# An RWKV-6 layer inside a sixteen-part kernel: one straight-line front, 32 scan units of 16 keys by 8 values, values spread by DMA, and a norm by a centring product

## The reference, cut to what matters

```python
delta = shifted - x                      # x one token back, minus x
xp = tanh((x + delta * mu0) @ W_x0.T)    # 160 columns, five groups of 32
mus = einsum(xp, W_x2) + x_bias          # one mix per kind: r, w, k, v, g
r, k, v, g = ((x + delta * mu) @ W.T)    # 64, 64, 128, 128 columns
w = tanh((x + delta * mu_w) @ W_w1.T) @ W_w2.T + b_w2
# per head h of 4, key i of 16, value j of 32, token t:
o[t, j] = sum_i r[t, i] * (S[i, j] + u[i] * k[t, i] * v[t, j])
S[i, j] = exp(-exp(w[t, i])) * S[i, j] + k[t, i] * v[t, j]
o = (o - mean) * rsqrt(var + eps)        # over the 32 values of a head
x = x + (o * gn_weight + gn_bias) * silu(g) @ W_o.T
```

## Time and profile before

| | |
|---|---|
| median of 3 runs | 3856.74 us (3844.39 to 3859.89) |
| the profiled execution, its own time | 3816.58 us |
| its span | 3814.8 us |
| granted clock of TensorE, mean | 0.864 |
| busy: PE, DVE, ACT, POOL | 3021.5, 2024.3, 1374.9, 670.1 us |
| from this layer's layernorm to its last sum | 2479.1 to 2832.1 us of the span |

### The profile page before, as it was taken

How to read it: one execution, slowest core, us unless ns; L and a number is a source line. 1 busy time by engine, 2 the same in 40 slices (tenths; PEclk the granted TensorE clock), 3 DMA queues, 4 the chain that set the end, 5 groups by cost and what they waited for, 6 DMA issues and landing times. The chain is left out here.

```text
span 3814.8 us, 57392 instructions
## 1 busy us (share of the span) xinstructions
PE 3021.5 (79%) x22522; PEld 1598.0 (42%) x22522; DVE 2024.3 (53%) x3730; ACT 1374.9 (36%) x2632; POOL 670.1 (18%) x561
## 2 busy tenths in 40 slices
PE   6566877788887699897688889977878658867986
PEld 4454247323475244444222224422233443654555
DVE  5211254588753788203788771166763453536643
ACT  3211434623243366423567762210102112223652
POOL 0000017065354100004443200000000000240003
PEclk9666869788888799999899999978789679977997
DMA  2022002022012321000311000000000000023202
GB/s 103 14 66 63 0 19 56 16 94 66 17 47 80 72 40 28 1 0 13 66 30 29 2 1 0 10 0 0 0 0 0 1 0 21 25 56 77 48 15 67
DMA packets 81292, 118.55 MB, mean 31 GB/s; under 512 B 12743, under 2 KB 51623, under 8 KB 79763
## 3 DMA queue, kind: packets, MB, share of 16 engines
q1 hardware_dynamic: 74003, 100.67, 10.6%
q0 software_dynamic: 7040, 14.43, 1.4%
HBM read 90.04 MB, written 24.81 MB: 30 GB/s over the span
## 5 line engine op out<-in xcount | busy, mean ns | idle before, releaser
L1674 DVE TENSOR_REDUCE at_mp<-PS 128x1 f32<-128x384 f32 (+3 forms) x640 | 313.3, 538 | 115.3 <-PE PS L1524 99.0
L1624 ACT ACTIVATE at_pt<-PS 128x384 f32<-128x384 f32 (+3 forms) x704 | 288.4, 456 | 212.8 <-PE PS L1536 177.6
L1521 PE MATMUL PS<-at_kx,at_qx 72*128 72x384 bf16 (+5 forms) x640 | 218.4, 346 | 67.7 <-DMA at_kx<-L_attn_a_parts 26.7
L1534 PE MATMUL PS<-at_qx,at_kx 105*128 105x512 bf16 (+5 forms) x704 | 214.8, 315 | 8.0 <-ACT at_pt L1624 6.0
L3860 ACT ACTIVATE ls_pt<-PS,ls_far 128x512 f32<-128x512 f32 x256 | 155.4, 684 | 23.1 <-PE PS L3681 18.6
L4007 DVE CUSTOM_DVE_ANT_0 PS<-PS,ls_pt 128x1024 f32<-128x1024 f32 x128 | 153.8, 1240 | 18.1 <-ACT ls_pt L3860 15.1
L2287 DVE TENSOR_TENSOR_SCAN mb_ring<-PS,mb_ring 128x1024 f32<-128x1024 f32 x64 | 146.6, 2291 | 18.9 <-POOL mb_ring L2226 6.7
L2242 PE MATMUL PS<-mb_ring,ident 128*128 128x512 f32 x256 | 147.7, 729 | 6.0 <-DVE mb_ring L2292 6.0
L1536 PE MATMUL PS<-at_above,identb 128*128 128x128 bf16 x704 | 134.1, 223 | 0.0
L2271 ACT ACTIVATE PS<-mb_dt,mb_a 128x1024 f32<-128x1024 f32 x64 | 71.6, 1118 | 168.1 <-DVE mb_ring L2287 168.1
L1521 PEld LDWEIGHTS PS<-at_kx,at_qx 102*128 102x128 bf16 (+1 forms) x640 | 64.5, 101 | 161.3 <-DVE at_mp L1674 85.6
(11 more groups left out here) (820 smaller groups left out, 6787.0 us busy)
## 6 DMA issues: line engine op xcount, KB each, us to landing
dl_arena<-in_fir_bank SPq DMA_DIRECT2D x32, 256.0 KB, 3.2
lnA<-mb_rows SPq DMA_DIRECT2D x16, 512.0 KB, 3.7
XN<-mb_rows SPq DMA_DIRECT2D x16, 512.0 KB, 3.7
ffn_place<-in_ffn_L SPq DMA_DIRECT2D x4, 1152.0 KB, 17.2
at_qx<-L_attn_a_parts SPq DMA_DIRECT2D x24, 192.0 KB
at_kx<-L_attn_a_parts SPq DMA_DIRECT2D x72, 64.0 KB
at_qx<-L_attn_b_parts SPq DMA_DIRECT2D x24, 192.0 KB
at_kx<-L_attn_b_parts SPq DMA_DIRECT2D x72, 64.0 KB
```

The costliest lines, as they stand in the source:

```text
L1521: mm = nc.tensor.matmul(PS[:, n % 3, 0:e - c], QX[0:RAW, u % 3, g, blk(i, P)], KX[0:RAW, u % 3, g, c:e], start=True, stop=True)
L1534: mm = nc.tensor.matmul(PS[:, 3 + n % 3, 0:e - c], KX[0:FULL, u % 3, g, blk(j, P)], QX[0:FULL, u % 3, g, c:e], start=True, stop=True)
L1624: nc.scalar.activation(PT[:, y % SLOTS, g, 0:e - c], PS[:, 3 + n % 3, 0:e - c], ACT.Exp, scale=SCALE).then_inc(exp_done, 1)
L1674: nc.vector.tensor_reduce(best, sc, AX.X, ALU.max).then_inc(s_maxed, 1)
```

## The change

Only `l2a` is changed. It has three stages in place of ten passes through five, no loop, and no split into bfloat16 parts:

- The front works on four blocks of 512 tokens. PE's order is a pipeline over steps s: `narrow` of block s, `mix` of s - 1, `project` of s - 2, `finish` of s - 3. ACT keeps the projections, POOL adds XN to each mix, and SP writes V to a DRAM tensor `rw_v_rows`.
- The recurrence has 32 units. A unit holds 16 keys by 8 values of one head on the 128 partitions, so four units in a row belong to one head and use the same spread of k, decay and r, made by float32 products with SEL once per head. SP fetches the 8 value rows, each to 16 partitions, in four buffers; POOL multiplies them by the spread key, which ACT has copied to SBUF; DVE scans and multiplies by r; PE sums the keys with a shifted 0/1 matrix RED, and at the end of a sequence adds the bonus VB.
- The norm works on four blocks of 512: a product with CM = I - BM centres, ACT takes Square, then Ln and Exp(-0.5 x) for the reciprocal root, DVE has two fused instructions and the sum.

POOL builds SEL (128 x 512 float32, two affine selects), RED (16 affine selects of 8 columns) and CM beside the layernorm.

```diff
+        arena = sb("rw_arena", [P, 20 * BLK])
...
+        KS = [k.XN[:, i * SEQ:(i + 1) * SEQ] for i in range(2)]
+        SS = [k.lnA[:, 0:SEQ], k.lnA[:, SEQ:2 * SEQ]]
...
+            own(pool.tensor_tensor(CM[:, :], k.ident[:, :], BM[:, :], ALU.subtract))
...
+            for d in range(DK):
+                own(pool.affine_select(out=v, in_=v, compare_op=ALU.not_equal, fill=1.0, base=-VG * d, pattern=[[-1, VG]], channel_multiplier=1))
...
+            @block.sync
+            def _(sp):
+                for b in range(NBLK):
+                    sp.wait_ge(p_kept, KINDS * b + V_KEPT)
+                    sp.dma_start(v_rows[:, blk(b)], V[:, blk(b)]).then_inc(stored, 16)
+                sp.wait_ge(stored, 16 * NBLK)
...
+                def narrow(b):
+                    pe.wait_ge(xx0_done, b + 1)
+                    if b:
+                        pe.wait_ge(xp_done, 2 * b)
...
+                for s in range(NBLK + 3):
+                    if s < NBLK:
+                        narrow(s)
+                    if 0 <= s - 1 < NBLK:
+                        mix(s - 1)
+                    if 0 <= s - 2 < NBLK:
+                        project(s - 2)
+                    if 0 <= s - 3 < NBLK:
+                        finish(s - 3)
...
+                        pool.wait_ge(mixed, KINDS * b + i + 1)
+                        pool.tensor_tensor(XX[:, b % 2, i, :], XX[:, b % 2, i, :], k.XN[:, blk(b)], ALU.add).then_inc(xx_done, 1)
...
+                for u in range(UNITS):
+                    s, j = u // GROUPS, u % GROUPS
+                    if u >= 4:
+                        sp.wait_ge(kv_done, u - 3)
+                    sp.dma_start(VS[u % 4], v_rows[VG * j:VG * j + VG, s * SEQ:(s + 1) * SEQ].unsqueeze(0).to_broadcast([DK, VG, SEQ])).then_inc(spread[u % 4], 16)
...
+                    if u >= 3:
+                        pool.wait_ge(scanned, u - 2)
+                    pool.tensor_tensor(KV[u % 3], VS[u % 4], KS[g % 2], ALU.mult).then_inc(kv_done, 1)
...
+                def decays(g):
+                    if g:
+                        pe.wait_ge(scanned, PER_HEAD * g)
+                    lines(g, 2, slice(64, P), RD[64:P, :], d_ready)
+
+                def receptance(g):
+                    if g:
+                        pe.wait_ge(sr_done, PER_HEAD * g)
+                    lines(g, 4, slice(0, 64), RD[0:64, :], r_ready)
...
+                for u in range(UNITS):
+                    g = u // PER_HEAD
+                    last = u % PER_HEAD == PER_HEAD - 1 and g + 1 < SPREADS
+                    if last:
+                        decays(g + 1)
+                        receptance(g + 1)
+                    add(u)
+                    if last and g + 2 < SPREADS:
+                        keys(g + 2)
...
+                    nc.vector.tensor_tensor_scan(SS[u % 2], wide(2), KV[u % 3], 0.0, ALU.mult, ALU.add).then_inc(scanned, 1)
+                    dve.wait_ge(scanned, u + 1)
+                    dve.wait_ge(r_ready, g + 1)
+                    if u >= 2:
+                        dve.wait_ge(o_added, u - 1)
+                    nc.vector.tensor_tensor(SR[u % 2][:, 1:], SS[u % 2][:, 0:SEQ - 1], wide(4)[:, 1:], ALU.mult).then_inc(sr_done, 1)
...
+                def root(b):
+                    act.wait_ge(var_ready, b + 1)
+                    if b >= 2:
+                        act.wait_ge(normed, b - 1)
+                    nc.scalar.activation(RS[:, b % 2, :], PS[:, 4 + b % 2, :], ACT.Ln, bias=k.eps_col[:, 0:1]).then_inc(log_done, 1)
+                    act.wait_ge(log_done, b + 1)
+                    nc.scalar.activation(RS[:, b % 2, :], RS[:, b % 2, :], ACT.Exp, scale=-0.5).then_inc(root_done, 1)
+
+                square(0)
+                square(1)
+                for b in range(NBLK):
+                    root(b)
+                    if b + 2 < NBLK:
+                        square(b + 2)
...
+                    nc.vector.scalar_tensor_tensor(out=O[:, blk(b)], in0=PS[:, b, :], scalar=W[pre + "gn_weight"], in1=RS[:, b % 2, :], op0=ALU.mult, op1=ALU.mult).then_inc(normed, 1)
```

More of the change, by code:

```diff
@@ new lines, in l2a @@
+        XX = rows(0, 10).rearrange("p (a i n) -> p a i n", a=2, i=KINDS)
+        DX, XX0, XP, XP5, RU = (rows(10 + 2 * i, 2).rearrange("p (a n) -> p a n", a=2) for i in range(5))
+        T64 = k.lnA[0:64, 0:2 * BLK].rearrange("p (a n) -> p a n", a=2)
+        VS = [rows(2 * i, 2) for i in range(4)]
+        KV = [rows(8 + 2 * i, 2) for i in range(3)]
+        SR = [rows(14 + 2 * i, 2) for i in range(2)]
+        KS = [k.XN[:, i * SEQ:(i + 1) * SEQ] for i in range(2)]
+        SS = [k.lnA[:, 0:SEQ], k.lnA[:, SEQ:2 * SEQ]]
@@ L2335, in layer_constants @@
+        O = V
+        SQ, RS = (rows(2 * i, 2).rearrange("p (a n) -> p a n", a=2) for i in range(2))
+        v_rows = nc.dram_tensor("rw_v_rows", (P, NTOK), F32).ap()
+        wide = lambda a: PS[:, a:a + 2, :].rearrange("p a b -> p (a b)")
         def layer_constants(pool, own):
-            own(pool.memset(XS[:, 0:1], 0.0))
-            own(pool.memset(SS[:, 0:1], 0.0))
             head_constants(k, pool, own, BM[:, :], 1.0 / 32)
+            own(pool.tensor_tensor(CM[:, :], k.ident[:, :], BM[:, :], ALU.subtract))
@@ L2340, in layer_constants @@
             own(pool.memset(SEL[:, :, :], 0.0))
-            v = SEL[:, :, :].rearrange("q d (h v) -> q d h v", v=32)
+            v = SEL[:, :, :].rearrange("q h (d v) -> q h d v", v=VG)
             for part in range(2):
-                own(pool.affine_select(out=v, in_=v, compare_op=ALU.not_equal, fill=1.0, base=-64 * part, pattern=[[-1, DK], [-DK, 4], [0, 32]], channel_multiplier=1))
+                own(pool.affine_select(out=v, in_=v, compare_op=ALU.not_equal, fill=1.0, base=-64 * part, pattern=[[-DK, HEADS], [-1, DK], [0, VG]], channel_multiplier=1))
@@ new lines, in l2a, with _, variance, out @@
+        with stage(nc, "centered", "squared", "var_ready", "log_done", "root_done", "normed", "gated", "y_ready", "added") as (
+                block, centered, squared, var_ready, log_done, root_done, normed, gated, y_ready, added):
+            @block.tensor
+            def _(pe):
+                def variance(b):
+                    pe.wait_ge(squared, b + 1)
+                    if b >= 2:
+                        pe.wait_ge(log_done, b - 1)
+                    nc.tensor.matmul(PS[:, 4 + b % 2, :], BM[:, :], SQ[:, b % 2, :], start=True, stop=True).then_inc(var_ready, 1)
+                def out(b):
+                    pe.wait_ge(gated, b + 1)
+                    if b >= 2:
+                        pe.wait_ge(added, b - 1)
+                    nc.tensor.matmul(PS[:, 6 + b % 2, :], W[pre + "W_o"], O[:, blk(b)], start=True, stop=True).then_inc(y_ready, 1)
+                for b in range(NBLK):
+                    nc.tensor.matmul(PS[:, b, :], CM[:, :], O[:, blk(b)], start=True, stop=True).then_inc(centered, 1)
+                variance(0)
+                variance(1)
+                for b in range(NBLK):
+                    if b + 2 < NBLK:
+                        variance(b + 2)
+                    out(b)
+            @block.scalar
+            def _(act):
+                def square(b):
+                    act.wait_ge(centered, b + 1)
+                    if b >= 2:
+                        act.wait_ge(var_ready, b - 1)
+                    nc.scalar.activation(SQ[:, b % 2, :], PS[:, b, :], ACT.Square).then_inc(squared, 1)
+                def root(b):
+                    act.wait_ge(var_ready, b + 1)
+                    if b >= 2:
+                        act.wait_ge(normed, b - 1)
[4 more added lines that the diff above has]
+                square(1)
+                for b in range(NBLK):
+                    root(b)
+                    if b + 2 < NBLK:
+                        square(b + 2)
+            @block.vector
+            def _(dve):
+                def norm(b):
+                    dve.wait_ge(root_done, b + 1)
+                    nc.vector.scalar_tensor_tensor(out=O[:, blk(b)], in0=PS[:, b, :], scalar=W[pre + "gn_weight"], in1=RS[:, b % 2, :], op0=ALU.mult, op1=ALU.mult).then_inc(normed, 1)
+                    dve.wait_ge(normed, b + 1)
+                    nc.vector.scalar_tensor_tensor(out=O[:, blk(b)], in0=O[:, blk(b)], scalar=W[pre + "gn_bias"], in1=G[:, blk(b)], op0=ALU.add, op1=ALU.mult).then_inc(gated, 1)
+                def add(b):
+                    dve.wait_ge(y_ready, b + 1)
+                    nc.vector.tensor_tensor(k.X[:, blk(b)], k.X[:, blk(b)], PS[:, 6 + b % 2, :], ALU.add).then_inc(added, 1)
+                norm(0)
+                for b in range(1, NBLK):
+                    norm(b)
+                    add(b - 1)
+                add(NBLK - 1)
+                dve.wait_ge(added, NBLK)
```

362 lines of the change are left out of this document (184 added, 178 removed).

## The result

The changed kernel takes 3735.87 us (median of 4 runs, 3731.93 to 3738.48) against 3854.88 us before: a ratio of 0.9691 (95% interval 0.9674 to 0.9707), 119.0 us less. Forecast were 3728 us and 3694 to 3774, so the range holds it. The stages are less well forecast than the total, since misses of opposite sign cancel in part: the front is 14 us over, the recurrence 8 under.

A forecast was written before the change was run, and what follows sets the result against it. The old recurrence was taken as not simply PE's, the front as held by serial hand-overs. Front 63, recurrence 137.7 and norm 23.1 make 223.8 against 353.0 us; 3856.7 - 129 gives 3728, range 3694 to 3774.

The forecast's parts named there:

- 5.2 us for half clock: Front: time added for PE at half clock, 1.7 us for the first product pair and 3.5 for a slow stretch.
- the high bound of 76: Front: upper limit of its forecast time, four blocks of 18 us in series; the low bound was 52.
- a front over 70 us: Front: a sign named beforehand that would show the prediction wrong.
- PE with pauses after the third step: Front: opposite of a sign for being right, which was PE without pauses from the third step.
- PE's trouble was the serial hand-over: Old front: PE's clock of 0.71 to 0.73 was put down to each product waiting for a serial hand-over between engines.
- in series, 76 us: Front: rival that in-order queues make the four blocks run in series, kernel 3741 us; chance 0.14.
- 6.7 + 115.2 + 11 + 4.8: Recurrence: start, 32 units of 3.60 us, stalls at seven changes of head, and tail; 137.7 us in all.
- The unit of 3.60: Recurrence: one scan and one product on DVE, 2.33 us from scan to product, then 1.27.
- The rival in which PE bounds this stage: Recurrence: PE at 1.2 GHz needs 24.4 us a head against 16; in part, kernel 3745 to 3795; chance 0.12.
- The seven loads of 1.28 us: Norm: each change between Ln and Exp on ACT costs a table load, 9.0 us in all.
- the lower of the two values: Constants on POOL beside the layernorm: the list of about 9 us costs nothing, or 1 us at its upper end.
- The offset of 40 us: Whole kernel: the median of the runs stands 40 us (1.05%) above the profiled execution, carried over to the forecast.

The follow-up runs named there:

- e12: Changed kernel with the edits of e2, e4, e5, e7, three unread products before the first narrow products, first decay ahead of second key: 3675.9 us, ratio 0.9608.
- e3: Changed kernel with six unread products in PE's early pauses, ahead of the front's first three narrow products: 3721.25 us, front 4.6 us shorter.
- e5: Changed kernel with the front's 32-row mix products zero-padded to 128 rows: 3727.45 us, front 69.7 us.
- e6: Changed kernel with eleven unread 128-row products in PE's pauses, at the front's start and among the mix products: 3724.6 us.
- e1: Changed kernel with the front's four blocks run one after the other instead of pipelined: 3725.24 us.
- e9: Changed kernel with the recurrence's key product moved from POOL to DVE: 3741.53 us beside a before of 3819.68, recurrence 171.2.
- e8: Changed kernel with every spread transfer of the recurrence issued twice and POOL waiting for both: 3772.2 us, recurrence 152.5.
- e7: Changed kernel with decay and key spreads changing banks from head to head, so the next decay is spread early: 3725.4 us, recurrence 125.9.
- e11: Changed kernel with each scan also waiting on the DVE product just before it: 3708.51 us beside 3819.68, recurrence 134.7.
- e10: Changed kernel with decay, receptance and key spread for every unit instead of once per head: 3795.44 us beside 3819.68.
- e4: Changed kernel with the norm's four Ln all before its four Exp, four buffers and banks: 3724.8 us, norm 20.8 instead of 25.3.
- e2: Changed kernel with all four difference blocks of the front made first on DVE, in four buffers: 3729.55 us.

## Why the prediction was right, and where it wasn't

The total was right within 8 us (3728 against 3735.9), the layer's saving 119 instead of 129; 2.7 of the missing 10 us are the layernorm's clock, which the sum had not considered.

**Front: the step that failed.** "5.2 us for half clock" (3.5 for the slow stretch, 1.7 for the first pair) was the mis-sized term. PE was busy 65.6 us. At full clock the same products would take 47 to 54 us, an estimate: 40 single ones, which follow each other every 0.95 us (and not 0.87), and 8 pairs at 1.13 make 47; e12's front at full clock had 57.2, of which three unread products are 2.9. So half clock cost 11 to 19 us where 5.2 were put down, and PE was idle 11.8 instead of some 9. The price at half clock was low too: the 1.7 us of the earlier trace rows are the mean of a pair whose second product already ran faster, and one product takes 2.07. The front lies above the high bound of 76 that I had set, though in the trace the four blocks do overlap. Two of the signs that I had named came out on the wrong side: a front over 70 us, and PE with pauses after the third step (3.52 us before `narrow(2)`). The argument that PE's trouble was the serial hand-over was right as far as the idle time goes, which shrank; the clock, though, stayed near where the earlier trace rows had it, 0.76 after 0.71 to 0.73, and I should have asked what would lift it. e3, e5, e6 and e12 show that it can be lifted: with PE's pauses filled or shortened, the front has 0.83 to 1.00, and in e12 it takes 59.2 us, less than the forecast 63. What in these edits lifts it, the pauses or the rows, stays open. The rival "in series, 76 us" had the length right and the reason wrong: e1 runs in series and is not slower.

**Recurrence: mechanism right, sizes off.** As forecast, DVE alone sets the unit (e9), POOL's product and the transfer are hidden (e8), PE's spread stalls DVE at the seven changes of head and nowhere else (e7). Its sum was 6.7 + 115.2 + 11 + 4.8; measured are 7.6 + 110.6 + 6.3 + 4.8 = 129.3. The unit of 3.60 was meant to be Mamba's, in which each scan waits on DVE's own last product, but no row has its 1.27 from product to scan: Mamba's timeline has 1.35 and a unit of 3.68. e11 puts this wait back and has 3.68 as well; the new kernel doesn't have it and takes 3.46. The change of head came to 0.9 and not 1.6 us, since the clock was 0.97 and not Mamba's 0.85. The rival in which PE bounds this stage did not come. Spreading once per head is what keeps PE out of it (e10: 222 us).

**Norm: right, but for its start.** The seven loads of 1.28 us came, and the two Squares and three roots took 12.8 us (12.9 forecast). The first Ln came 5.1 us after the stage's start and not 3.4: PE does all four centring products, 3.67 us, before the first variance. By the rule of the Trainium skill (ScalarE: Activation LUTs, section "Table sets: the hidden batching unit"), which has ln and exp in one set, there would be no load between them; here each change has one, and e4 gains 4.5 us by having only one change.

**Constants: nothing, as the lower of the two values had it.** POOL ended 11.3 us after the layernorm's start, 2 us later than before, but still ahead of the layernorm: in e1, where it ran at full clock, its last instruction ended 11.5 us after the start, as in before. After's 14.2 go with its clock of 0.82.

**The offset of 40 us** between profile and median was carried over rightly, but as a guess. Most of it lies in the two stretches of other sublayers named above. They took about 652 and 520 us in before's trace and in e9 to e12 (beside a before of 3819.68 us), and 662 to 672 and 534 to 541 in after and e1 to e8. e1 to e8 ran beside a before of 3850 us, on other chips than e9 to e12. Why a chip should differ there, no run shows.

## What to carry to other kernels

Price a product by the clock that its stretch will have, and don't take for granted that a change of order lifts it: in this front, with pauses of 1 to 4 us between products, the mean clock of 0.76 means about half of the time at 1.2 GHz, and padding products to 128 rows, making their inputs earlier and adding a few products that nobody reads made it 18 us shorter. Put work on the engine that has time, not on the one that does it fastest (e9). And wait on the count that the data needs, not on the instruction just issued (e11).

## What the hardware showed beyond that

- DVE began a scan before the duration of the product ahead of it was over, where it had no wait for it: 1.14 us from start to start with a product that is given 1.22 (after), 1.35 with a wait for that product (e11).
- Two DVE instructions with both inputs in SBUF took more than twice as long beside POOL's sums of two SBUF tiles. POOL was at work until 2537.90 and from 2545.46 to 2552.23 here:

```profile
2536.66 1.78 DVE L2477 TENSOR_TENSOR rw_arena<-XN 128x511 f32<-128x511 f32 x1
2538.48 0.75 DVE L2481 SCALAR_TENSOR_TENSOR rw_arena<-rw_arena,small_L,XN 128x512 f32<-128x512 f32 x1
...
2550.42 0.69 DVE L2477 TENSOR_TENSOR rw_arena<-XN 128x512 f32<-128x512 f32 x1
2551.15 1.64 DVE L2481 SCALAR_TENSOR_TENSOR rw_arena<-rw_arena,small_L,XN 128x512 f32<-128x512 f32 x1
```

  The same subtraction takes 1.78 at 2536.66 and 0.69 at 2550.42, the fused instruction behind it 0.75 and 1.64. With the differences ahead of POOL's sums (e2) DVE is busy 2.1 us less. Why the subtraction at 2550.42 was spared, although POOL was at work, stays open. The scans and products of the recurrence have one input in PSUM and take 2.29 and 1.22 us with POOL or without it (e9).
- Two products on different 32-row groups overlap: two in 1.13 us at full clock, against 1.02 for one.
- The clock differs between executions of the same code: the unchanged front had 0.72 to 0.79 and 74.5 to 79.5 us. One execution of such a stage settles nothing under 3 us.
